# Recommendation tower on one core: linear products of block 2 ahead, the last unit's biases paired, a maximum in place of two bias products, and unit 15's norms ahead of unit 14's projection

## What is computed

```python
x = layer_norm(dense @ Wd.T, gd, bd)                     # one row of 128 per sample
y = layer_norm(einsum('bnd,ed->bne', rows, Ws), gs, bs)  # 26 rows of 128
y = layer_norm(einsum('bne,pn->bep', y, Wsi), gsi, bsi)  # 32 rows of 128
T = concat([x, y])                                       # 33 rows
Z = T @ T.T                                              # 33 x 33, the part below the diagonal is kept
z = layer_norm(Zflat @ Wl.T, gl, bl)[:384]
h = max(concat([z, dense]) @ W_top1 + b_top1, 0)
h = max(h @ W_top2 + b_top2, 0)
out = h @ W_top3
```

## Time and profile before

| | |
|---|---|
| median of the runs shown | 170.69 us |
| the profiled execution's own time | 172.12 us |
| its span | 170.3 us |
| PE / DVE / ACT / POOL busy | 83 / 77 / 58 / 60 % |
| last gather issued, its rows used by PE | 134.0 us, 137.0 us |

### The profile page before, as it was taken

One profiled execution on the slowest core, in us unless ns is written; L12 is line 12 of the kernel. 1 busy time (PEld: TensorE's weight loads), 2 busy tenths in 40 slices (PEclk: granted clock), 3 DMA queues, 4 the chain that ended last, 5 costly groups with the idle time before them and its releaser, 6 DMA issues.

```text
span 170.3 us, 4661 instructions
## 1 busy us (share of the span) xinstructions
PE 141.4 (83%) x1819; PEld 105.9 (62%) x1819; DVE 130.5 (77%) x303; ACT 98.5 (58%) x245; POOL 102.4 (60%) x112
## 2 busy tenths in 40 slices
PE   0199876987796869896979998978899989999995
PEld 0084543634353557483967684948696848788994
DVE  6379769795949997898498995966899969784262
ACT  0303334888755868786488685744766767551140
POOL 3777777777777777777777777777777500021000
DMA  4923616142211113211111231111112300101000
GB/s 133 341 42 91 261 31 208 34 115 58 37 27 30 24 23 81 52 34 24 29 31 29 52 73 30 26 28 27 30 27 67 66 8 0 38 16 29 0 0 0
DMA packets 6009, 9.59 MB, mean 56 GB/s; under 512 B 2309, under 2 KB 3544, under 8 KB 5860
## 3 DMA queue, kind: packets, MB, share of 16 engines
q0 software_dynamic: 3424, 3.46, 11.1%
q1 hardware_dynamic: 2232, 5.08, 9.4%
q10 hardware_dynamic: 332, 0.76, 1.2%
HBM read 8.01 MB, written 0.00 MB: 47 GB/s over the span
## 4 chain that ended last, share of the span: by engine, by line
POOL 49%; PE 19%; issue 18%; DVE 8%; ACT 3%; DMA 3%; DVEq 0%; ACTq 0%
POOL g_sb L262 48%; PE psW L359 3%; PE psB L325 2%; PE psB L379 2%; DVE B L849 2%; DVE ssB L856 1%; DMA g_sb<-in_table,row_id 1%; PE psU L306 1%; PE psZ L431 1%; PE psG L291 1%; DMA ids_sb<-in_ids 1%; PE psZ L340 1%; PE psH L379 1%; DVE T L869 1%; PE psW L404 1%
## 5 line engine op out<-in xcount | busy, mean ns | idle before, releaser
L262 POOL DMA_INDIRECT g_sb<-in_table,row_id x104 | 100.4, 965 | 31.7 <-issue 31.4
L849 DVE TENSOR_TENSOR B<-psB,bias 128x512 f32<-128x512 f32 x31 | 20.0, 686 | 13.5 <-PE psB L325 12.5
L306 PE MATMUL psU<-wsi_x,g_sb 128*128 128x192 f32 (+4 forms) x128 | 21.2, 309 | 5.9 <-DVE g_sb L842 5.7
L306 PEld LDWEIGHTS psU<-wsi_x,g_sb 128*128 128x128 f32 x128 | 19.0, 190 | 11.0 <-DVE g_sb L842 11.0
L653 ACT ACTIVATE Zs<-psZ 32x264 f32<-32x264 f32 x59 | 22.3, 378 | 1.1
L625 ACT ACTIVATE sqB<-B 128x512 f32<-128x512 f32 x31 | 18.7, 629 | 6.7 <-DVE B L849 6.7
L869 DVE TENSOR_TENSOR T<-B,psG 128x512 f32<-128x512 f32 x31 | 21.3, 686 | 1.1
L856 DVE TENSOR_REDUCE ssB<-sqB 128x16 f32<-128x512 f32 x32 | 21.7, 677 | 0.1
L325 PE MATMUL psB<-U,ws_g 64*128 64x512 f32 x64 | 18.1, 641 | 3.9 <-ACT U L614 3.7
L291 PEld LDWEIGHTS psG<-gram,sT 128*128 128x128 f32 x104 | 12.8, 191 | 10.3 <-ACT sT L601 10.0
L291 PE MATMUL psG<-gram,sT 128*128 128x128 f32 x104 | 15.9, 291 | 0.7 <-ACT sT L601 0.7
(11 more groups left out here) (161 smaller groups left out, 220.7 us busy)
## 6 DMA issues: line engine op xcount, KB each, us to landing
g_sb<-in_table,row_id POOLq DMA_INDIRECT x104, 2.5
wl_sb<-in_wl SPq DMA_DIRECT2D x1, 1280.0 KB, 5.4
w_sb<-in_w SPq DMA_DIRECT2D x2, 512.0 KB, 4.4
w_sb<-in_w SPq DMA_DIRECT2D x1, 768.0 KB, 4.2
small_sb<-in_small SPq DMA_DIRECT2D x1, 615.5 KB, 4.0
dense_sb<-in_dense ACTq DMA_DIRECT2D x1, 512.0 KB, 6.2
Zt<-Zs SPq DMA_DIRECT2D x3, 80.0 KB
Zt<-Zs SPq DMA_DIRECT2D x3, 70.0 KB
```

The costliest lines, as they stand in the source:

```text
L262: pool.indirect_dma_start(g_sb[:, k, h * DSP:(h + 1) * DSP], None, table, bass.IndirectOffsetOnAxis(row_id[:, 2 * k + h:2 * k + h + 1], 0) ...
L306: mm = pe.matmul(psU[:, (lo - US * j) * PROJ:(hi - US * j) * PROJ], g_sb[:, SLOTS * b + c, :], wsi_x[:, c, lo - s0:hi - s0, :], start=(n = ...
L849: dve.tensor_tensor(B[:, h, :].rearrange("p (s j) -> p s j", j=PROJ), psB[h][:, :].rearrange("p (s j) -> p s j", j=PROJ), bias[:, :].rearr ...
```

## The change

1. `linear(2, 0, 10)` of step 14 is split: its first four products are issued right behind `mix(14)`, ahead of `transposes(15)`, and the six others stay where the ten were. The waits for `d_zt` and `h2_ready` go with the first four.
2. In step 14 unit 15's first norm moves ahead of work of unit 14, on PE (`norms(15)` ahead of `project(14)`), on DVE and on ACT.
3. The bias of unit 15 is put into both halves in PSUM by a pair of products with 64 rows each (only one of them not zero). `add_b(15,1)` goes away, and `squares_b`, `norm_b` of unit 15 read PSUM for both halves. The pair waits for both `add_b(14,h)`.
4. In `last_block`, max(p + b sd, 0) is written as max(p, -b sd) + b sd. DVE makes `least` = -b sd and both maxima. The two products with one row (457) go away, and one product with one row, (W_top3 · b_top2) times sd, stands ahead of the last output product.
5. `keep_z(15,2)` moves from DVE to ACT, and ACT's `third_squares(1)` goes behind two `keep_z`.
6. At the start, two small products make W_top3 · b_top2, and `bs_rows` is 128 rows.

```diff
-EARLY, ALL = (9, 9, 10), FLIN // P * CW
+AHEAD, EARLY, ALL = (0, 0, 4), (9, 9, 10), FLIN // P * CW
...
@@ PE project(u)
-                    pe.wait_ge(B_added, 2 * u - 1)
-                    pe.matmul(psB[0][:, :].rearrange("p (s j) -> p s j", j=PROJ), bs_sb[0:1, 0:E],
-                              wsum[:, :].rearrange("p (o j) -> p o j", o=1).broadcast_to([1, US, PROJ]),
-                              start=True, stop=False)
+                    pe.wait_ge(B_added, 2 * u)
+                    for h in range(2):
+                        hs = slice(h * DSP, (h + 1) * DSP)
+                        pe.matmul(psB[h][:, :].rearrange("p (s j) -> p s j", j=PROJ), bs_sb[hs, :],
+                                  wsum[hs, 0:PROJ].rearrange("p (o j) -> p o j", o=1).broadcast_to([DSP, US, PROJ]),
+                                  start=True, stop=False)
...
@@ PE last_block
-                for f in range(K2):
-                    pe.matmul(psO[f][:, 0:BS], bs_sb[0:1, E + f * P:E + (f + 1) * P], zsd[0:1, :], start=True,
-                              stop=False)
...
+                pe.matmul(psY[0:1, 0:BS], wsum[0:1, PROJ:PROJ + 1], zsd[0:1, :], start=True, stop=False)
...
@@ PE step(t)
                 mix(t)
+                if late and j == 0:
+                    linear(b, 0, AHEAD[b])
                 if t + 1 < UNITS and not behind(t + 1):
                     transposes(t + 1)
+                if t == UNITS - 2:
+                    norms(t + 1)
                 project(t)
...
-                    linear(b, 0, EARLY[b])
+                    linear(b, AHEAD[b], EARLY[b])
...
@@ ACT step(t)
+                if t == UNITS - 2:
+                    deviation_a(t + 1)
                 squares_b(t, 0)
                 squares_b(t, 1)
                 enter_x(t)
-                if t + 1 < UNITS:
+                if t + 1 < UNITS - 1:
                     deviation_a(t + 1)
...
@@ DVE last_block
+                for f in range(K2):
+                    dve.tensor_scalar(least[:, f, :], zsd[:, :], b2_c[:, f:f + 1], -1.0, ALU.mult,
+                                      ALU.mult).then_inc(least_ready, 1)
...
+                    dve.tensor_tensor(h2T_last[:, f * BS:(f + 1) * BS], psO[f][:, 0:BS], least[:, f, :],
+                                      ALU.max).then_inc(h2T_f[f], 1)
...
@@ DVE step(t)
-                if t < UNITS - 1:
+                if t == UNITS - 2:
+                    mult_a(t + 1)
+                    sums_a(t + 1)
                     add_b(t, 0)
-                add_b(t, 1)
-                if t + 1 < UNITS:
+                    recip_a(t + 1)
+                    scale_a(t + 1)
+                    add_b(t, 1)
+                elif t < UNITS - 2:
+                    add_b(t, 0)
+                    add_b(t, 1)
                     mult_a(t + 1)
                     sums_a(t + 1)
                 if late and j == 0 and b:
                     copy_y(b - 1)
                 sums_b(t, 0)
-                if t + 1 < UNITS:
+                if t + 1 < UNITS - 1:
                     recip_a(t + 1)
                     scale_a(t + 1)
                 sums_b(t, 1)
```

More of the change, by code:

```diff
@@ L325, in project @@
                     pe.matmul(psB[h][:, :], ws_g[h * DSP:(h + 1) * DSP, :], U[h * DSP:(h + 1) * DSP, u % 2, :],
-                              start=not (last and h == 0), stop=True).then_inc(B_done, 1)
+                              start=not last, stop=True).then_inc(B_done, 1)
             def inner(u):
@@ L353, in linear @@
                         pe.wait_ge(m_kept, 1)
[L354 removed]
+                elif b == LAST - 1 and hi == ALL:
                     pe.wait_ge(y_copied, b)
@@ L531, in _ @@
             pe.wait_ge(w_prep, 5)
-            pe.matmul(psU[0:1, 0:PROJ], sel_sb, wsi_c[:, 0, :], start=True, stop=True).then_inc(wsum_done, 1)
+            pe.matmul(psU[:, 0:PROJ], sel_sb.broadcast_to([P, P]), wsi_c[:, 0, :], start=True, stop=True)
+            for k in range(K2):
+                mm = pe.matmul(psU[:, PROJ:PROJ + 1], w3_c[:, k:k + 1].broadcast_to([P, P]), b2_c[:, k:k + 1],
+                               start=(k == 0), stop=(k == K2 - 1))
+            mm.then_inc(wsum_done, 1)
             dense_part(0)
@@ L536, in _ @@
             pe.wait_ge(wsum_ready, 1)
-            pe.matmul(psU[:, 0:PROJ], bs_sb[:, 0:E], wsum[:, :], start=True, stop=True).then_inc(bias_done, 1)
+            pe.matmul(psU[:, 0:PROJ], bs_sb[0:DSP, :], wsum[0:DSP, 0:PROJ], start=True, stop=True).then_inc(bias_done, 1)
             transposes(0)
@@ L699, in _ @@
             act.wait_ge(wsum_done, 1)
-            act.activation(wsum[:, :], psU[0:1, 0:PROJ], ACT.Copy).then_inc(wsum_ready, 1)
+            act.activation(wsum[:, :], psU[:, 0:PROJ + 1], ACT.Copy).then_inc(wsum_ready, 1)
             act.wait_ge(x_stat, 2)
@@ L788, in _ @@
                 step(t)
-            keep_z(UNITS - 1, 0)
-            keep_z(UNITS - 1, 1)
+            for gq in range(3):
+                keep_z(UNITS - 1, gq)
             deviation_w(LAST - 1)
@@ L860, in recip_b @@
                 dve.wait_ge(B_sd, 2 * u + h + 1)
-                r = rB_last[:, :] if u == UNITS - 1 and h == 0 else rB[:, h, :]
+                r = rB_last[:, h, :] if u == UNITS - 1 else rB[:, h, :]
                 dve.reciprocal(r, sdB[:, h, :]).then_inc(B_recip, 1)
@@ L1158 @@
     ws2 = np.concatenate([x["L0_rec_Ws"].T, x["L0_rec_Ws"].T])
+    bs_rows = np.zeros((P, E), np.float32)
+    for h in range(2):
+        bs_rows[h * DSP] = x["L0_rec_bs"]
     arrays = {
```

42 lines of the change are left out of this document (22 added, 20 removed).

## The result

The changed kernel took 173.77 us in the median (173.48 to 174.03, four runs), the kernel before 170.80 us (170.27 to 171.25, four runs). The recorded ratio is 1.0145, 95% interval [1.0109, 1.0181]: slower, and more so than forecast (172.3, range to 173.0). The quotient of the two medians is larger, 1.0174; how the recorded ratio is weighed is not on record. The profiled execution took 174.03 us, its span is 172.2 us (170.3 before).

What follows compares the result with a forecast made beforehand. Gathers on POOL were taken to set the pace until about 111 us, then PE, DVE and ACT alone. Terms 1.29 + 0.30 = 1.59 on 170.69 gave 172.3 us, range 171.0 to 173.0.

Steps and rivals of the forecast that it cites:

- The term 1.29: Step 14 to inner(15): project(15) 1.49 us late, the paired squares give back 0.20, so inner(15) is 1.29 late.
- slower still: Rival at the early linear products: block 2's Z lands 0.5 us later, at 137.4, and PE waits; 172.8 us; chance 0.08.
- faster: Rival at PE's idle time before the last gather: h2_ready by 136.10 lets early products fill it; -0.8, 169.9 us; chance 0.08.
- nothing measurable: Rival at keep_u(15): ACT's queue doesn't hold U, the copy follows mix(15); 0.4 us in all, 171.1 us; chance 0.16.
- ACT, the term that decides: ACT in step 14: squares wait for the late add_b(14,1), so keep_u(15) waits some 1.2 us in ACT's queue, starting at 145.94.
- the end, 0.30: Last block: the new one-row product ahead of the last output product costs 0.30 us, between 0.22 and 0.40.
- the paired bias, 0.20: Unit 15's squares: without add_b(15,1) they run as a pair at once, which gives back 0.20 us.
- I forecast 170.69 + 1.6: Whole kernel: the summed cost of 1.6 us added to the 170.69 us median of the runs, giving 172.3 us.
- the sum 1.59: Whole kernel: 1.29 us from step 14 plus 0.30 at the end, start work costed at 0.

Runs made afterwards that it cites:

- e12: The changed kernel measured again without any edit: 172.95 us, ratio 1.0106 against the kernel before.
- e13: The changed kernel with DVE's add_b(14,1) back ahead of recip_a(15) and scale_a(15): ratio 1.0149 against the kernel before.
- e15: e13 with DVE's copy of block 1's output moved behind the first copy of the linear sums in step 15: ratio 1.0151 against the kernel before.
- e6: The changed kernel with unit 15's copy of psU on ACT ahead of unit 14's second root and unit 13's last Z copy: ratio 1.0123 against the kernel before.
- e14: The changed kernel with the edits of both e13 and e6, the early addition and the early copy: ratio 1.0164 against the kernel before.
- e2: The changed kernel without the four early linear products, so with the reordering alone of the two moves: ratio 1.0054 against the kernel before.
- e7: e4 with the new one-row product issued ahead of the last block's second layer, where PE is idle: ratio 0.9984 against the kernel before.
- e4: The changed kernel with neither the early linear products nor the reordering of step 14: ratio 1.0024 against the kernel before.
- e11: The kernel before with only the paired bias and the moved Z copies, b_top2 in a transfer of its own: 170.58 us, ratio 0.9972.
- e1: The kernel before, measured and profiled once more without any edit: 171.50 us, ratio 1.0009.
- e5: The changed kernel measured again without any edit: 173.55 us, ratio 1.0124 against the kernel before.
- e10: The kernel before with only the two small products at the start added, their result unused: ratio 1.0017.
- e9: The changed kernel without the two small products at the start: ratio 1.0109 against the kernel before.
- e8: The kernel before with the first dense products computed once more at the start, into an unused bank: ratio 1.0010.

## Why the prediction was right and wrong

**Right: step 14.** With the 0.13 us by which unit 14's copy came later taken off (136.87 - 136.74), the changed kernel has the last transposes done at 138.45 (forecast 138.36), the norms at 139.97 (139.91), the scaling at 142.64 (142.56), the addition of half 1 at 143.25 (143.17), unit 15's copy at 145.94 (145.94), its projection at 146.59 (146.59), the second half of `inner(15)` at 151.49 (151.50). The term 1.29 came out at 1.28 (14.75 - 13.47). Z was the last to release the early products in the profile (137.12, forecast 136.89); in e12 and e13 it was the store by ACT, at the same 0.25 us behind the copy. Z landed at 137.02, half a us later than the 136.5 worked out, but the store ended at 136.98 (136.35 + 0.63), so this cost next to nothing. So "slower still" did not come to pass (its 137.4 is half a us behind 136.89, not behind 136.5), and "faster" and "nothing measurable" fell with the times above. The agreement is not luck: it holds at each point of the way, not only in the sum.

**Right as a time, not as the cause: "ACT, the term that decides".** In the changed kernel ACT's queue holds unit 15's copy as forecast. It has no idle time from the second square of unit 14 (143.41) to the copy (146.07), and the activations between the two take 2.03 us (144.04 to 146.07) where 2.10 was taken. (The prediction speaks of six activations; the rows that it adds up are seven.) But the late addition ahead of them is worth 0.13 us (e13), not the 1.2 by which the prediction has the copy wait: without it ACT waits for DVE's sums instead. What releases ACT is DVE in either case. DVE starts step 14 1.46 us later (3.27 against 1.81 behind the copy) and then, in the changed kernel and in e13, runs without a gap up to zT; 0.20 us taken out of its queue there gave 0.20 everywhere behind (e15). The prediction had the row for it, DVE's idle time of 1.32, and counted only that `mult_a(15)` starts 0.20 later. It left out that the two additions ahead of it no longer fill the time before the norms, so that DVE idles 2.78 us. In the table zT is copied 6.5 to 6.9 us behind DVE's first instruction in every kernel but e6 and e14, where DVE waits for the root that the copy has passed. The reordering brings the rows of unit 15 earlier (scaled 4.65 behind the copy in e2, 5.82 before), but PE, which in e2 waits 1.06 us for ACT's copy of the transposes and then has the same ten products, starts `mix(15)` no earlier (6.43 in e2, 6.07 before). Whether fewer activations on ACT behind DVE's sums would also give something was not tried.

**Wrong in size: the end, 0.30.** It was 0.46 (4.33 or 4.34 against 3.88 from the first activation of the last block's first layer to the end of DVE's last product). 0.39 of it lies between the two pairs of output products, 0.07 ahead of them; both are gone in e7. The 0.07 belongs to the two one-row products that the prediction let go for 0: with a product of one row just ahead of it the second layer starts 0.47 behind that activation (before and e7), without one 0.57 (166.26 to 166.83). The one-row product starts 0.53 behind the first pair and the second pair 0.30 behind the row, where the pairs are 0.44 apart without it. I took the middle between the two bounds, and the upper one, 0.40, was right for the row itself. The Trainium skill, TensorEngine Tiling (Array Packing), section Tiling Modes, says that a change of tiling mode drains TensorE. By that rule, if the one-row product is another mode, the term was 0.40; the trace agrees with 0.39, but does not name the mode.

**Right: the paired bias, 0.20.** From the start of `project(15)` to the second half of `inner(15)` it is 4.90 us in the changed kernel (146.72 to 151.62) and 5.11 before (145.10 to 150.21): 0.21 less. Alone, with part 5, the pair gives more, 0.41 (e4 and e11, 13.04 against 13.45 in e1), 0.09 of it because `project(15)` itself starts earlier there (8.25 against 8.34).

**The step that failed: "I forecast 170.69 + 1.6", with nothing for the stretch ahead of unit 14's copy.** Behind the copy the sum 1.59 was too small by the end term alone: 1.28 + 0.46 = 1.74, and the traces have 1.74 to 1.77. That is part of the 2.97 us between the two medians. The other 1.2 us lies ahead of the copy. There the prediction put part 6 at 0, since the wait for gathers covers it, and "some tenths" without that cover; the range allows it nothing. This rest is not steady. By the same subtraction it is 0.4 us in e5 (173.55 - 171.42 - 1.77) and none in e12 (172.95 - 171.21 - 1.77). So the runs do not show that it comes from the change, and its cause stays open. Three things on record bear on it.

First, the cover can be used up: in e2, e6 and e10 the chain holds no gather, and unit 14 comes up to about 1 us later. e10 has this with the two start products alone, but its median shows no more than 1.0017 [0.9991, 1.0042], and the first profile of the changed kernel had no late start (unit 0's copy at 24.93). Second, that profile had a stretch of lower granted clock:

```profile
60.00:80.00 20.00, 16.71 (x215) 12.39 (x213) 16.59 (x39) 15.22 (x37) 15.12 (x17) 0.91 0.23 44
```

The same stretch in e12 (columns: stretch, length, busy us and count of PE, PE's weight loads, DVE, ACT, POOL, granted clock, DMA share, GB/s):

```profile
60.00:80.00 20.00, 17.02 (x220) 12.38 (x219) 17.27 (x40) 16.18 (x38) 15.12 (x17) 1.00 0.22 44
```

0.91 is a mean over the stretch: part of it was at 1.2 GHz, the rest at 2.4 GHz. Unit 14's copy came 0.95 us later than in e12 (136.87 against 135.92). Such stretches were in four profiled executions (the first of the changed kernel, e9, e14, e15), with unit 14's copy at 136.87 to 137.50. But of the four timed runs of the first comparison only the profiled one had a mean granted clock of 0.99, so this does not carry their median. Nor does the change seem to make such stretches more frequent: 11 of 108 runs of the kernel before and 1 of 16 of the changed kernel had a mean of 0.99 or less. e12 and e14, one and the same program up to step 14, had ratios as far apart as 1.0106 and 1.0164; three of e14's six runs were at 0.99 and none of e12's, but its other three (172.58 to 173.74 us) do not bring the ratio down to e12's. Third, the base: the forecast was added to a median of three runs, 170.69, where larger samples of the kernel before gave 171.0 to 171.5. A sum of 1.76 on those is 172.8 to 173.3, around the end of the range.

## What to carry to other kernels

When an instruction is moved ahead on one engine, look at what the next engine did in the meantime: the order of PE that brought one chain forward took away the work with which DVE had filled its wait, and a queue without gaps passes on its start in full. Take away a named wait in an experiment before believing in it, and look in the trace of that experiment at what the moved instruction has passed: here one wait gave way to the next after 0.13 us, and the other was only traded for a wait on the root. Forecast from more than three runs, and give the range what executions of one kernel differ by. A single one-row product belongs where TensorE is idle, not between the last products of the path.

## What the runs showed that was not expected

- A one-row product with one column of weights between two output products cost 0.46 us of the path (e7 against the changed kernel), although its two passes add up to 0.37 us busy.
- Four passes of 512 columns at the start took 3.76 us in some executions and 1.96 in others (e10, e12). In e2 and e6, which have the long form, the records of the full clock begin only behind these passes (19.31 and 19.25 us; 12.92 in e12).
- 1.8 us of extra products at the start cost nothing that the ratio shows (e8, first copy 0.9 us later than in e1). Of four executions with a first copy later than 27 us, three had no gather on the path at all.
